# Second cross-attention of a Perceiver block: twelve units, not eight, by ScalarE and GpSimd, one ring of eight slots, squares of two units

## The reference

```python
rq = (iQ @ Wq.T).reshape(b, q, H, ADIM)                    # H = 16, ADIM = 8
kv = (iK @ Wkv.T).reshape(b, s, 2, H, ADIM)
scores = jnp.einsum('bqhd,bshd->bhqs', rq, rk) / sqrt(ADIM)
scores = jnp.where(mask[:, None, :, :], jnp.float32(-1e+32), scores)
t = jax.nn.relu(scores + nbias[0])
t = t * t
attn = t / (t.sum(-1, keepdims=True) + IEPS)
o = jnp.einsum('bhqs,bshd->bqhd', attn, rv).reshape(b, q, H * ADIM)
return o @ Wo.T
```

## Time and profile before

| | before |
|---|---|
| runs | 448.31, 449.05 and 448.26 us; median 448.31 |
| span of the profiled execution, first to last instruction | 445.9 us |
| stage in question, from its first score to the last copy of an output | 322.38 to 396.62, 74.24 us |
| TensorE busy over the span | 408.6 us, 92% |
| VectorE, ScalarE, GpSimd busy over the span | 333.9, 272.1, 223.9 us |

### The profile page before, as it was taken

How to read it: one execution, slowest core, us unless ns; L and a number is a source line. 1 busy time by engine, 2 the same in 40 slices (tenths; PEclk the granted TensorE clock), 3 DMA queues, 4 the chain that set the end, 5 groups by cost and what they waited for, 6 DMA issues and landing times.

```text
span 445.9 us, 8251 instructions
## 1 busy us (share of the span) xinstructions
PE 408.6 (92%) x3222; PEld 338.5 (76%) x3222; DVE 333.9 (75%) x518; ACT 272.1 (61%) x398; POOL 223.9 (50%) x134
## 2 busy tenths in 40 slices
PE   8987999999989999998998886999799999975996
PEld 6865999999978999998986355664578888853795
DVE  4799899888878988884735847505889999953764
ACT  4577788777778777776522463210189999943244
POOL 0133799997789888865402482000066646500024
PEclk9999999999999999999999996999989999999899
DMA  6949877879997797877940000999940000010000
GB/s 213 278 124 206 195 179 166 193 178 207 210 210 160 174 204 166 190 168 234 424 167 0 2 0 0 212 204 197 242 202 1 4 3 1 3 32 0 0 2 12
DMA packets 19510, 59.81 MB, mean 134 GB/s; under 512 B 5904, under 2 KB 7696, under 8 KB 18064
## 3 DMA queue, kind: packets, MB, share of 16 engines
q1 hardware_dynamic: 19472, 59.30, 53.9%
HBM read 19.30 MB, written 0.13 MB: 44 GB/s over the span
## 4 chain that ended last, share of the span: by engine, by line
PE 56%; DVE 14%; SPq 8%; issue 7%; DMA 6%; ACT 6%; POOL 1%; POOLq 0%; ACTq 0%; DVEq 0%
SPq L533 6%; PE ps L635 6%; PE ps L637 6%; PE ps L636 6%; PE ps L613 5%; PE ps L614 5%; PE ps L615 5%; DMA kstack<-k_lo 4%; PE ps L993 3%; PE ps L899 3%; PE ps L920 3%; DVE w_ring L1576 3%; DVE max L1422 3%; DVE y_sq L1412 2%; PE ps L568 2%
## 5 line engine op out<-in xcount | busy, mean ns | idle before, releaser
L386 POOL TENSOR_TENSOR dT_lo<-z_sq,dT_hi 128x1024 fp32r<-128x1024 f32 x56 | 133.3, 2402 | 31.1 <-ACT dT_hi L1022 31.0
L1087 ACT ACTIVATE y_sq<-ps,nmax 128x1024 f32<-128x1024 f32 x64 | 70.8, 1112 | 40.7 <-DVE nmax L1451 38.6
L1422 DVE TENSOR_REDUCE max<-ps 128x1 f32<-128x1024 f32 x64 | 77.9, 1218 | 19.7 <-PE ps L615 19.6
L635 PE MATMUL ps<-dT_hi,ctx_hi 128*128 128x256 f32 x256 | 74.3, 290 | 1.9 <-POOL dT_lo L386 1.9
L1412 DVE STREAM_TRANSPOSE y_sq<-y_sq 128x1024 f32<-128x1024 f32 x60 | 74.0, 1234 | 0.0
L637 PE MATMUL ps<-dT_hi,ctx_lo 128*128 128x256 f32 x256 | 72.4, 283 | 0.0
L636 PE MATMUL ps<-dT_lo,ctx_hi 128*128 128x256 f32 x256 | 72.3, 283 | 0.0
L1576 DVE SCALAR_TENSOR_TENSOR w_ring<-ps,neg_nbias,cap 128x1024 f32<-128x1024 f32 x56 | 67.6, 1277 | 3.1 <-PE ps L899 3.1
L1228 ACT ACTIVATE p_ring<-w_ring,nbias_sb 128x1024 f32<-128x1024 f32 x56 | 62.2, 1146 | 1.9 <-DVE w_ring L1576 1.2
L1022 ACT ACTIVATE dT_hi<-z_sq 128x1024 fp32r<-128x1024 f32 x60 | 61.5, 1059 | 2.7 <-PE ps L637 2.5
L613 PE MATMUL ps<-ctxT_hi,qk_hi 128*128 128x512 f32 x128 | 52.5, 410 | 3.7 <-ACT y_sq L1087 3.5
(11 more groups left out here) (210 smaller groups left out, 653.4 us busy)
## 6 DMA issues: line engine op xcount, KB each, us to landing
z_sq<-y_sq SPq DMA_DIRECT2D x240, 128.0 KB, 2.4
w_sb<-in_w SPq DMA_DIRECT2D x2, 2048.0 KB, 15.7
kstack<-k_hi SPq DMA_DIRECT2D x8, 512.0 KB, 10.5
kstack<-k_lo SPq DMA_DIRECT2D x8, 512.0 KB, 12.0
ctx_raw<-in_ctx_nat SPq DMA_DIRECT2D x8, 256.0 KB, 7.9
ctxT_raw<-in_ctx_t SPq DMA_DIRECT2D x1, 2048.0 KB, 8.9
wg_sb<-in_wg SPq DMA_DIRECT2D x1, 1088.0 KB, 13.2
wu_sb<-in_wu SPq DMA_DIRECT2D x1, 1088.0 KB, 16.1
```

Of the source, the lines that this page charges most:

```text
L386: return engine.tensor_tensor(d_ring(dT_lo, m), z_chunk(m), d_ring(dT_hi, m), ALU.subtract)
L635: mm(acc, hi[:, k, :], dT_hi[m % 3][:, cols], start=(k == 0), stop=False)
L1087: nc.scalar.activation(out_t, keys, ACT.Exp, bias=nmax[:, hs % 2:hs % 2 + 1], scale=SCALE0, accum_out=rowsum[:, hs, p:p + 1]).then_inc(exp ...
L1422: return v.tensor_reduce(max2[:, 2 * (hs % 2) + p:2 * (hs % 2) + p + 1], slot(2 * hs + p), AX.XY, ALU.max)
```

## The change

Every sixteen units now hold three, not two, that go over ScalarE and GpSimd, and they are spread evenly: units 0, 5, 10, 16, 21, 26, 32, 37, 42, 48, 53, 58 (`POOLED`). VectorE does the other 52, not 56. One ring of eight slots, `p_ring`, replaces `w_ring` and the old `p_ring`: VectorE writes the relu there, and ScalarE squares it in place, two neighbouring slots in one operation of 2048 columns, 26 in all. VectorE's wait is now that the unit eight places earlier in the ring has been weighed. The weighing of a ring unit comes six steps after its score, that of a pooled unit nine. ScalarE issues the relu of a pooled unit m ahead of a square that ends with unit m-1, and copies a combo's accumulator nine units after the combo's last score. The mask `keep` has two more slices for the other units that can be pooled, so six small operations compute it, not one. GpSimd spreads the queries about a combo ahead, as before.

```diff
+RING = 8
...
-        w_ring = A.take("w_ring", (P, 3, 1024))
-        p_ring = A.take("p_ring", (P, 3, 1024))
-        w_first = A.take("w_first", (P, 1024))
+        p_ring = A.take("p_ring", (P, RING, 1024))
...
-        WEIGH_LAG = 3
+        POOLED = tuple(16 * i // 3 for i in range(3 * NU // 16))
+        LAG_RING, LAG_POOL = 6, 9
...
+        def weigh_step(m):
+            return m + (LAG_POOL if m in POOLED else LAG_RING)
+        weigh_order = sorted(range(NU), key=weigh_step)
+        def weighed(m):
+            return weigh_order.index(m) + 1
+        def of_combo(c):
+            return [m for m in weigh_order if m // UNITS == c]
+        def ring_no(m):
+            return m - sum(k < m for k in POOLED)
+        ring_units = [m for m in range(NU) if m not in POOLED]
...
@@ TensorE @@
                 if m >= 3:
-                    if is_first(m - 3):
-                        pe.wait_ge(relu_done, c_of(m - 3) + 1)
+                    if m - 3 in POOLED:
+                        pe.wait_ge(relu_done, POOLED.index(m - 3) + 1)
                     else:
-                        pe.wait_ge(w1_done, nth(m - 3))
+                        pe.wait_ge(w1_done, ring_no(m - 3) + 1)
...
-            for m in range(0, NU + WEIGH_LAG + 1, 2):
-                for i in range(2):
-                    if m + i < NU:
-                        scores1(m + i)
-                for i in range(2):
-                    if 0 <= m + i - WEIGH_LAG - 1 < NU:
-                        weigh_v(m + i - WEIGH_LAG - 1)
+            for step in range(0, NU + LAG_POOL, 2):
+                for m in (step, step + 1):
+                    if m < NU:
+                        scores1(m)
+                for m in weigh_order:
+                    if weigh_step(m) in (step, step + 1):
+                        weigh_v(m)
...
@@ ScalarE @@
+            def relu_pooled(m):
+                n, at = POOLED.index(m), 2 * (m % 3)
                 act.wait_ge(s1_psum, m + 1)
+                if n:
+                    act.wait_ge(sq_pool, n)
+                nc.scalar.activation(w_pool[:].rearrange("p (a n) -> p a n", a=2), ps[:, at:at + 2, :], ACT.Relu,
                                      bias=nbias[:]).then_inc(relu_done, 1)
+            relu_pooled(0)
             for m in range(NU):
+                if m % UNITS == 1 and m >= 2 * UNITS:
+                    copy_o1(m // UNITS - 2)
+                if m + 1 in POOLED:
+                    relu_pooled(m + 1)
+                if m in POOLED or ring_no(m) % 2 == 0:
                     continue
+                n = ring_no(m)
+                act.wait_ge(w1_done, n + 1)
+                two = p_ring[:, (n - 1) % RING:(n - 1) % RING + 2, :].rearrange("p r n -> p (r n)")
+                nc.scalar.activation(two, two, ACT.Square, bias=nbias[:]).then_inc(sq_done, 1)
...
@@ GpSimd @@
+            for n, m in enumerate(POOLED):
+                while spread < COMBOS and spread * UNITS <= m + UNITS + 1:
+                    spread_q(nc.gpsimd, spread).then_inc(qbd_pool, 1)
+                    spread += 1
+                pool.wait_ge(relu_done, n + 1)
+                heads = w_pool[:].rearrange("p (h n) -> p h n", h=4)
+                nc.gpsimd.tensor_tensor(heads, heads, bc(keep_of(m), 1, 4), ALU.mult).then_inc(kept, 1)
+                pool.wait_ge(kept, n + 1)
+                if n:
+                    pool.wait_ge(pv1_done, weighed(POOLED[n - 1]))
+                nc.gpsimd.tensor_tensor(p_pool[:], w_pool[:], w_pool[:], ALU.mult).then_inc(sq_pool, 1)
...
@@ VectorE @@
-                if at > 3:
-                    dve.wait_ge(sq_done, at - 3)
+                if n >= RING:
+                    dve.wait_ge(pv1_done, weighed(ring_units[n - RING]))
```

More of the change, by code:

```diff
@@ L199, in build @@
         oT1 = A.take("oT1", (P, 2 * 4, S))
-        keep = A.take("keep", (P, B, 2 * S))
+        keep_last = A.take("keep_last", (P, B, 2 * S))
         A = Arena(nc, probs_at + B * (H // 2) * S * 4, qk_at)
@@ L278, in build @@
         q1s = A2.take("q1s", (P, 4, T), F32R)
-        p_first = Arena(nc, attn0_at, stage).take("p_first", (P, 1024))
+        p_pool = Arena(nc, attn0_at, stage).take("p_pool", (P, 1024))
         A = Arena(nc, attn0_at + B * H * DH * 4, wo0_at)
@@ L284, in build @@
         wq1 = A.take("wq1_sb", (P, 4, P))
+        w_pool = Arena(nc, attn0_at + B * H * DH * 4, wo0_at).take("w_pool", (P, 1024))
         mask_sb = Arena(nc, wo0_at, stage).take("mask_sb", (P, B * NBLK, S), U8)
+        keep_two = Arena(nc, wo0_at, stage).take("keep_two", (P, 2, B, 2 * S))
         ps = ctx.enter_context(nc.psum_tensor("ps", [P, 8, 512], F32))
@@ L901, in scores1, with weigh_v @@
                 last.then_inc(s1_psum, 1)
-            def weigh_v(n):
-                c, u = n // UNITS, (n + 1) % UNITS
+            def weigh_v(m):
+                c, u = m // UNITS, m % UNITS
                 b, g = c // 4, c % 4
-                if u == 1 and c >= 2:
+                first, last_of = of_combo(c)[0] == m, of_combo(c)[-1] == m
+                if first and c >= 2:
                     pe.wait_ge(o1_copied, c - 1)
-                if u == 0:
-                    pe.wait_ge(sq_pool, c + 1)
-                    p = p_first[:]
-                else:
-                    at = nth(c * UNITS + u)
-                    pe.wait_ge(sq_done, at)
-                    p = p_ring[:, (at - 1) % 3, :]
+                if m in POOLED:
+                    pe.wait_ge(sq_pool, POOLED.index(m) + 1)
+                    p = p_pool[:]
+                else:
+                    pe.wait_ge(sq_done, ring_no(m) // 2 + 1)
+                    p = p_ring[:, ring_no(m) % RING, :]
                 for i in range(2):
@@ L921, in weigh_v @@
                                   p[:, (2 * j + i) * S:(2 * j + i + 1) * S],
-                                  start=(k == 2), stop=(k == 1))
+                                  start=(first and i == 0), stop=(last_of and i == 1))
                 last.then_inc(pv1_done, 1)
@@ L1341, in _ @@
             pool.wait_ge(keep_done, 1)
[L1342 to L1351, removed]
+            spread = 1
+            for n, m in enumerate(POOLED):
[9 more added lines that the diff above has]
+                nc.gpsimd.tensor_tensor(p_pool[:], w_pool[:], w_pool[:], ALU.mult).then_inc(sq_pool, 1)
             for e in range(E1 + 1):
@@ L1553, in _ @@
             dve.wait_ge(cap_done, 1)
-            v.tensor_scalar(keep[:], cap[:].rearrange("p (b k) s -> p b (k s)", b=B)[:, :, 0:2 * S], neg_nbias[:],
-                            None, ALU.is_gt).then_inc(keep_done, 1)
+            for b in range(B):
+                caps = cap[:, b * NBLK:(b + 1) * NBLK, :].rearrange("p k s -> p (k s)")
+                for m in (0, 3, 5):
+                    s = v.tensor_scalar(keep_of(4 * b * UNITS + m), caps[:, 2 * m * S:2 * (m + 1) * S], neg_nbias[:], None,
+                                        ALU.is_gt)
+            s.then_inc(keep_done, 1)
             for part, ready in ((slice(0, 1), 1), (slice(1, 4), 2)):
@@ L1565, in _ @@
             dve.wait_ge(load["kstack"], 256)
[L1566 to L1569, removed]
+            for n, m in enumerate(ring_units):
+                c, u = m // UNITS, m % UNITS
                 dve.wait_ge(s1_psum, m + 1)
-                if at > 3:
-                    dve.wait_ge(sq_done, at - 3)
+                if n >= RING:
+                    dve.wait_ge(pv1_done, weighed(ring_units[n - RING]))
                 k = (c // 4) * NBLK + 2 * u
```

35 lines of the change are left out of this document (7 added, 28 removed).

## The result

The changed kernel takes **451.71 us** (median of 17 runs, 449.45 to 454.44), the one before 449.05 in the same session (17 runs, 446.75 to 450.71): ratio 1.0066, 95% interval 1.0044 to 1.0087, so 2.0 to 3.9 us slower. Forecast were 450.5 and +2.2. Between kernels the stage is compared, from its first score to the end of its last output copy; the single profiles differ elsewhere too (with nearly the same code ahead of it, the stage began anywhere from 321.6 to 326.2 us), so the whole time is judged by runs alone.

The account below looks back on a forecast made before the run. TensorE was taken as the floor, at most 0.20 us a combo to gain. Terms 4.3 - 1.4 + 0.2 - 1.5 + 0.6 = +2.2 us on the median 448.31 gave 450.5 us, range 447.2 to 452.6.

Parts of the forecast that it names:

- The mechanism and the sign: TensorE stands at the score line because relus come late, so the kernel gets slower: +2.2 us; chance 0.56.
- Late relus: At the score line, scores three units after pooled ones wait for PSUM because ScalarE's relus start late; +4.3 us.
- Waits for squares: TensorE's wait of 0.20 us per combo for ScalarE's squares goes with the longer lags; -1.4 us.
- Start: Stage start: first weighings come two scores later, so scores wait for VectorE; +0.2 us, between 0 and +1.2.
- End: Stage end: fewer weighings ahead of unit 63's score, -1.5 us; a longer tail behind it, +0.6 us.
- Keep operations: Six mask operations for one on VectorE, covered by idle time and the kstack wait: no cost; 0.3 us uncovered.
- (a): Rival: ScalarE reaches even pooled units' relus in time, the 4.3 vanish; sum -2.1, 446.2 us, faster; chance 0.15.
- (b): Rival: ScalarE's square of two saves nothing, 2.08 instead of 1.90 us; about +1.6 more, 452.1 us; chance 0.08.
- (c): Rival: TensorE's clock falls to half rate over the new start; 1.7 us lost, 452.2 us; chance 0.05.

## Why the prediction was right, point by point

The mechanism and the sign were right, and the size came near: +2.2 forecast, +2.7 by the runs (2.0 to 3.9). That it came so near is partly luck. Two terms of the sum were too small, both the same way: the stage grew by 3.66 at full clock, 1.5 more than forecast, and the whole time showed 1.0 less of it than the stage. Two rows of the changed kernel bear on the first term, of ScalarE and of VectorE:

```profile
330.40 3.89 ACT L1238 ACTIVATE p_ring<-p_ring,nbias_sb 128x2048 f32<-128x2048 f32 x2
...
338.64 2.48 DVE L1590 SCALAR_TENSOR_TENSOR p_ring<-ps,neg_nbias,cap 128x1024 f32<-128x1024 f32 x2 [0.37 <-PE ps L917]
```

Measured against the stage at full clock:

- **Late relus**, +4.3 forecast. Lateness of S(13), S(19), S(29), S(35), S(45), S(51), S(61), from the timeline: 0.8, 0.4, 1.2, 0.4, 0.7, 0.4, 1.2, together **5.0**. Units 26 and 58 are exact, the others were 0.1 to 0.3 short. The squares are not to blame. Two that nothing holds up last 3.89, so they follow each other at 3.89 - 2.00 = 1.89, as forecast. Of the three between relu(10) and relu(16) (5.91) the last starts 0.1 late, at 339.96, when VectorE has finished unit 14 (338.64 + 1.28 = 339.92), whose score the late S(13) had put off: a stall hands part of itself on to the next relu. From relu(16) to relu(48) there are 378.85 - 341.87 = 37.0 us (36.3 forecast, 35.0 before).
- **Waits for squares**, -1.4: gone in every combo; one of 0.4 is left at the end, in the list of waits above. This term and the one before can be read together without naming a wait: from S(8) to S(63), with the same work, the change takes 394.16 - 330.56 = 63.60 and the kernel before 391.49 + 0.57 - 331.92 = 60.14, which is +3.46 where 4.3 - 1.4 = 2.9 was forecast.
- **Start**, +0.2 forecast, between 0 and 1.2: this term was mis-sized. S(8) begins 331.92 - 323.92 = 8.0 after S(0) in the second profile of the kernel before, with four weighings ahead, 7.60 in the change with one. Less three weighings at 0.50 that is **+1.1**. I sized it from the idle time in a stretch in which the clock was 0.50 for 3 us; slow scores hid the waiting for VectorE there. The row with the clock stood beside it and I used it for a rival alone. That the longer lag is the cause shows with a lag of four: 332.49 - 324.55 = 7.94 with three weighings, by the same working +0.4, where the same version with a lag of six has 7.50 with one, +1.0.
- **End**: 55 weighings ahead of S(63) instead of 58, -1.5 as forecast; from S(63), at 393.59 + 0.57 = 394.16, to the end at 400.34 there are 6.2, to the tenth (+0.6).
- **Keep operations**, 0: they end under the wait for `kstack`, which is still what starts the stage (2.5 us of idle ahead of S(0)).
- Together 5.0 - 1.4 + 1.1 - 1.5 + 0.6 = 3.8, or 3.7 with the 3.46; measured 3.66.

The rivals. (a), relus in time, did not happen; what it was worth show the versions that come near it, 73.26 with squares of two and 72.18 with single ones. (b), squares of two that save nothing, falls: they last 2.002 us and hold ScalarE for 1.89. The Trainium skill (ScalarE: Activation LUTs, What ACT_TABLE_LOAD costs) gives about 1990 ns for an operation with a bias by pointer at 2048 columns; the trace agrees within 12 ns. (c), the clock, was wrong for the change's profile, which shows 1.00 throughout the stage, but real: two of the eight other profiles that start with a lag of six or eight have it, at 1.36 us (1.7 forecast). The rule of the Trainium skill that GpSimd should not do such work (GPSIMD Engine Reference, section Engine selection) does not decide the time here: GpSimd is the slower engine in the trace too (4.29 us a unit, 1.28 on VectorE), but the four moved units do not lose, they gain 3.4 us (74.85 to 71.41) with two buffers and single squares.

Of the whole times one thing stays open. The version with two buffers and the earlier relu has a stage 0.5 shorter than that of the kernel before, and its runs are 0.1 to 2.0 us slower. Part of it goes with the clock. Each run's mean granted clock is on record, and its time goes with it: among the change's 17 runs the shortest, 449.45 us, has 0.990, and the three longest, 453.66 to 454.44, have 0.977. The runs of this version have 0.9814 in the mean, those of the kernel before on that chip 0.9836, and either kernel's runs are 0.19 to 0.30 us longer for each 0.001 less (a line fitted to each); that makes 0.4 to 0.7 of the 0.9 us between their means, an estimate. The rest stays open.

## What to carry to other kernels

An engine's slack by busy time says nothing of a hand-over with a deadline: here ScalarE and VectorE became less busy, TensorE's work stayed, and the stage became 3.7 us longer, mainly because a longer operation stood in the queue ahead of the one that frees PSUM, and because that one waited for a single buffer. When a stage is bound by a ring of few slots, work out for each slot what stands ahead of its release on the releasing engine, and what buffer that release waits for itself; cure both together, since an earlier place in the order without a second buffer only blocks the queue. The cure was two buffers in turn, worked in place with no further memory, and with them either an earlier relu (stage 73.26) or single squares (72.18); whether the fixed cost that squares of two save is worth anything beside that stays open.

## What was not expected of the hardware

TensorE's granted clock fell to half, 1.2 GHz, for about three microseconds in some executions and not in others. The kernel before has it over the first scores in one profile (0.50 from 323.0 on), and not in the other, though TensorE had stood idle just ahead of the stage in both, 1.8 and 2.2 us; two kernels of the change's family have it about 6.5 us into the stage, after five microseconds of which TensorE was busy 0.54 to 0.77 each, but for one of 0.99; the start stayed at 1.00 in the seven other profiles of kernels with a lag of six. With a lag of four, where the first weighings come sooner, neither of two profiles shows it; that is too few to say that it prevents it. A drop can cost 1.36 us, or only 0.5 where TensorE would have waited anyway, so a single profile's stage is not to be trusted to a microsecond before the clock's column has been read.
